# A fused attention block: the gate weight's eight factors summed on GpSimd instead of TensorE, under a newly written order of steps

## The chip, the cores and the metric

The kernel runs on one core of a Trainium2 chip. Its time is the device time of one execution in microseconds (us), the median over runs. The engines are TensorE (PE, matmuls), VectorE (DVE), ScalarE (ACT), GpSimd (POOL) and the DMA queues; each takes its instructions strictly in the order in which they are written and waits on semaphores.

## The reference

x has 4 batches of 512 rows of 256 numbers. What matters of it:

```python
xn = _layernorm(x, axis=-1)
qkv = xn @ Wqkv.T + bqkv          # 16 heads of 16; rotary embedding on q and k
att = softmax(causal(q @ k.T / 4)); s = (att @ v) @ Wo.T + bo
mixed = jnp.einsum('btd,rde->bte', xn, factors) / math.sqrt(8) + bias   # factors: 8 x 256 x 256
out = x + s * silu(mixed)
```

The einsum over r multiplies xn by the sum of the eight factors, so the kernel sums them once, at the start, into one 256x256 "gate weight".

## The kernel before

**Data.** All products with weights are made in two parts, a rounded high part (ACT copies it) and the rest (DVE or POOL subtracts): three products each. This holds for the weights of q and k (`wqk_sb`), of v and gate together (`wvg_sb`), of the output (`wo_sb`), for the normalised input (`xnT`) and for q and k themselves. Rotated q and k lie in `parts`; DMAs copy their high and low parts into stacked tiles `stack_q` and `stack_k`, whose free rows are filled by memsets beforehand (`fill`). For each batch the heads come in two units of eight.

**Steps.** For each batch: `stats` and `rstd` (mean and variance on DVE, the root on POOL), `normalise` (ACT; in batch 0 half on DVE), `turn_x` (PE transposes), `project_qk` (four steps of six products of 128x512), `rotate`, `high`, `low` and `stack` per unit, `project_vg` (four steps of six products), `maxima` (products for the row maxima, 40 chunks, reduced by DVE), `shift`, `scores` (products for the exponentials, taken by ACT), `values`, `take_o`, `turn_o`, `turn_y`, `project_o`, `store`.

**The gate weight.** Two DMAs load the factors into `fac`, a view of the tile `probs`, which is still free then. The step `sum_factors` adds the eight factors on PE by products with the identity into one PSUM bank; `split_gate` takes that bank: ACT writes the high part into `wvg_sb` (L910), DVE the rest (L792). `project_vg` of batch 0 needs both.

**The order.** `plan()` sorts the steps by the times written in the tables `CHAINS` (one row per batch), `MAXIMA`, `ATTENTION` and `END`. These times are only sort keys. Every engine walks the same sorted list and emits its own part of each step, so a step's place in the list sets what it stands behind on each engine. PSUM is used as a ring of eight banks in the order of the steps in `RING_KINDS`. `JOINED` names pairs of chunks whose masks are issued behind both chunks' products; `VALUES_AT` says at which chunk of the next group `values`, `take_o` and `turn_o` of a group stand.

**The stack of batch 0, unit 0.** It is filled through three queues (`FIRST_QUEUES`): the high and low parts of q by SP (step `stack` 0 and 1), the high part of k by POOL's queue (step `stack_gpsimd`), the low part of k by ACT's queue (step `stack_scalar`). These DMAs are issued by the engine itself at that place of its order. PE's first `maxima` waits for all of them (`wait_stack`):

```python
                eng.wait_ge(s_first_stack[0], 16 * first_dmas(SCALAR))
                eng.wait_ge(s_first_stack[1], 16 * first_dmas(GPSIMD))
            eng.wait_ge(s_stack[b % PARITIES][u], 16 * (STACK_DMAS * (b // PARITIES + 1) - others))
```

At the start PE runs 24 products of no use (`WARM_UP`, L570), and five more in `keep_warm` (L612).

Of the kernel before, what the change touches and what calls it, by code (L numbers as in the profile page):

```python
# [133 lines left out]
def attention_steps(b, g):  # L134

    s = []
    before = b * GROUPS + g - 1
    gb, gg = before // GROUPS, before % GROUPS
    for c in range(EXP_CHUNKS):
        s.append((c, ("scores", b, g * EXP_CHUNKS + c)))  # L140
        if before >= 0:
            s += [(c, (kind, gb, gg)) for kind, at in VALUES_AT if at == c]
    return s


def spread(steps, start, end):

    return [(start + (end - start) * (c // 2 * 2) / EXP_CHUNKS, step) for c, step in steps]


def shift_pairs(kind, b, u):
# [6 lines left out]
    (("stats", 0, -35.009), ("late_fill", 3, -22.829), ("rstd", 0, -21.238), ("keep_warm", 0, -14.711),  # L158
     ("split", 0, -14.601), ("normalise", 0, -14.545), ("fill", 0, -12.703), ("turn_x", 0, -11.842),
     ("turn_x", 1, -10.913), ("project_qk", 0, -10.001), ("split", 1, -9.814), ("fill", 1, -9.381),  # L160
     ("project_qk", 1, -9.255), ("rotate", 0, -9.216), ("stack_gpsimd", 0, -8.100), ("load", 1, -7.481),
     ("split", 2, -7.317), ("high", 0, -6.524), ("split", 3, -5.832), ("sum_factors", 0, -4.773),
     ("load", 2, -4.163), ("low", 0, -3.927), ("split_gate", 0, -2.954), ("stack_scalar", 1, -2.356),
     ("project_qk", 2, -2.146), ("fill", 2, -2.030), ("project_qk", 3, -1.952), ("rotate", 1, -1.795),
     ("stack", 0, -1.785), ("project_vg", 0, -1.389), ("high", 1, -0.567), ("project_vg", 1, -0.436),
     ("fill", 3, -0.397), ("low", 1, -0.384), ("project_vg", 2, -0.311), ("project_vg", 3, -0.259),
     ("stack", 1, 0.162), ("bias_vg", 0, 0.292), ("stack", 2, 0.735), ("first_shift", 0, 1.188),
     ("gate_tanh", 0, 1.232), ("shift", 0, 1.353), ("gate", 0, 1.431), ("stack", 3, 1.518), ("shift", 1, 1.896),
     ("turn_y", 0, 2.372), ("turn_y", 1, 2.604), ("project_o", 0, 2.816), ("project_o", 1, 2.903),
     ("load", 3, 3.163), ("store", 0, 4.465), ("store", 1, 7.296)),  # L170
    (("stats", 0, -6.753), ("rstd", 0, -3.783), ("normalise", 0, -1.479), ("turn_x", 0, 0.740), ("turn_x", 1, 0.776),
     ("project_vg", 0, 1.044), ("project_qk", 0, 1.089), ("project_qk", 1, 1.193), ("project_vg", 1, 1.225),
     ("project_vg", 2, 1.299), ("rotate", 0, 1.358), ("project_qk", 2, 1.522), ("project_qk", 3, 1.543),
     ("high", 0, 1.554), ("rotate", 1, 1.598), ("low", 0, 1.694), ("stack", 0, 1.705), ("project_vg", 3, 1.712),
     ("bias_vg", 0, 1.759), ("stack", 1, 1.867), ("gate_tanh", 0, 1.952), ("high", 1, 2.031), ("stack", 2, 2.043),
     ("low", 1, 2.173), ("shift", 0, 2.223), ("gate", 0, 2.292), ("stack", 3, 2.320), ("shift", 1, 3.016),
     ("turn_y", 0, 4.363), ("turn_y", 1, 4.820), ("project_o", 0, 5.177), ("project_o", 1, 5.617),
     ("store", 0, 12.675), ("store", 1, 13.830)),
    (("stats", 0, -1.348), ("rstd", 0, 0.743), ("normalise", 0, 1.650), ("turn_x", 0, 1.764), ("turn_x", 1, 1.774),
     ("project_qk", 0, 1.960), ("project_qk", 1, 1.985), ("project_qk", 2, 2.227), ("rotate", 0, 2.228),  # L180
     ("high", 0, 2.305), ("project_qk", 3, 2.315), ("stack", 0, 2.437), ("low", 0, 2.531), ("stack", 1, 2.635),
     ("rotate", 1, 3.021), ("project_vg", 0, 3.042), ("high", 1, 3.097), ("project_vg", 1, 3.223),
     ("project_vg", 2, 3.520), ("project_vg", 3, 3.563), ("low", 1, 3.580), ("bias_vg", 0, 3.581),
     ("shift", 0, 4.264), ("stack", 2, 4.352), ("gate_tanh", 0, 4.364), ("gate", 0, 4.716), ("stack", 3, 4.751),
     ("shift", 1, 5.306), ("turn_y", 0, 7.016), ("turn_y", 1, 7.279), ("project_o", 0, 7.661),
     ("project_o", 1, 7.690), ("store", 0, 16.049), ("store", 1, 22.818)),
# [927 lines left out]
```

## Time and profile before

| | |
|---|---|
| median of 3 runs | 225.77 us (225.0 to 225.97) |
| the profiled execution | 225.08 us, of which the span of its instructions is 223.3 us |
| PE busy | 210.4 us, 94% |
| DVE busy | 167.8 us, 75% |
| ACT busy | 137.9 us, 62% |
| POOL busy | 112.8 us, 51% |

The span runs from the first instruction to the last. A share of busy time is an average over stages that have different limits, so the stages at the start have to be read apart.

### The profile page before, as it was taken

The page shows a single profiled execution, that of the slowest core. Times are in us where ns is not written, and L with a number is a line of the kernel's source. Part 1 is how long each engine was busy: PE and PEld are TensorE (multiplying, and loading weights), DVE is VectorE, ACT ScalarE, POOL GpSimd, SP SyncE. Part 2 cuts the span into 40 slices and gives each one's busy share as a digit, 9 for nine tenths or more (in the row PEclk, how much of TensorE's full clock was granted, in tenths as well). Part 3 has the DMA queues.
Part 4 walks back from the last instruction along what each step waited for, and adds up shares of the span by engine and source line. Part 5 has one row for each costly group of instructions (what it writes and reads, how often), then busy time and mean ns, then how long its engine had stood idle before and what let it go on. Part 6 is the DMA issues. An engine that isn't in the chain of part 4 may idle for free.

```text
span 223.3 us, 5566 instructions
## 1 busy us (share of the span) xinstructions
PE 210.4 (94%) x2193; PEld 141.0 (63%) x2193; DVE 167.8 (75%) x268; ACT 137.9 (62%) x268; POOL 112.8 (51%) x104
## 2 busy tenths in 40 slices
PE   6999998998999999999999999999999999999892
PEld 2478866666657556667775575658756665585471
DVE  7779949979999797786976699669947796741233
ACT  2333461359664875893558978891278658869930
POOL 7884999753930860400779200954750034029912
PEclk9999999999999999999999999999999999999999
DMA  5996915101520340150036300035155000002002
GB/s 147 365 358 205 218 53 193 44 3 42 176 71 9 130 155 6 58 203 27 4 101 207 126 3 6 0 117 181 43 188 191 3 6 3 3 9 94 3 0 97
DMA packets 15790, 21.47 MB, mean 96 GB/s; under 512 B 2068, under 2 KB 9236, under 8 KB 15764
## 3 DMA queue, kind: packets, MB, share of 16 engines
q1 hardware_dynamic: 15248, 20.06, 27.5%
q0 software_dynamic: 192, 0.52, 1.0%
q10 hardware_dynamic: 324, 0.52, 0.8%
q8 instruction: 18, 0.29, 0.6%
q14 instruction: 8, 0.07, 0.1%
HBM read 6.16 MB, written 2.10 MB: 37 GB/s over the span
## 4 chain that ended last, share of the span: by engine, by line
PE 66%; DVE 18%; POOL 7%; ACT 4%; issue 4%; DVEq 0%; POOLq 0%
PE ring_ps L484 16%; DVE rowmax L832 10%; PE ring_ps L550 9%; PE ring_ps L521 9%; PE ring_ps L607 6%; PE ring_ps L626 5%; PE ring_ps L494 5%; PE ring_ps L502 5%; PE ring_ps L676 3%; PE ring_ps L642 2%; ACT probs L944 2%; PE ring_ps L681 2%; DVE parts L805 2%; PE ring_ps L583 1%; DVE by_sin L807 1%
## 5 line engine op out<-in xcount | busy, mean ns | idle before, releaser
L832 DVE TENSOR_REDUCE rowmax<-ring_ps 128x2 f32<-128x768 f32 (+3 forms) x103 | 89.5, 915 | 22.6 <-PE ring_ps L502 22.2
L944 ACT ACTIVATE probs<-ring_ps 128x512 f32<-128x512 f32 x160 | 83.5, 608 | 23.3 <-PE ring_ps L502 16.6
L484 PE MATMUL ring_ps<-probs,vaug 128*17 128x256 f32 (+3 forms) x528 | 37.8, 426 | 1.0 <-ACT probs L944 0.7
L521 PE MATMUL ring_ps<-stack_k,stack_q 62*128 62x512 f32 (+3 forms) x256 | 37.2, 355 | 1.6 <-DVE rowmax L832 0.6
L550 PE MATMUL ring_ps<-stack_q,stack_k 64*128 64x128 f32 (+3 forms) x256 | 36.4, 351 | 0.5
L502 PE MATMUL ring_ps<-ident_bf,masks 64*128 64x128 bf16 (+1 forms) x640 | 36.0, 210 | 0.0
L521 PEld LDWEIGHTS ring_ps<-stack_k,stack_q 62*128 62x128 f32 x256 | 20.9, 185 | 11.1 <-issue 7.8
L714 POOL TENSOR_TENSOR parts<-parts 128x1024 fp32r<-128x1024 f32 x7 | 16.7, 2381 | 21.9 <-ACT parts L915 21.9
L484 PEld LDWEIGHTS ring_ps<-probs,vaug 128*17 128x17 f32 x528 | 13.8, 97 | 22.0 <-issue 16.5
L550 PEld LDWEIGHTS ring_ps<-stack_q,stack_k 64*128 64x128 f32 x256 | 21.1, 185 | 8.9 <-issue 6.3
L626 PE MATMUL ring_ps<-wvg_sb,xnT 128*128 128x512 f32 x96 | 25.1, 405 | 1.2 <-DVE rowmax L832 0.8
L502 PEld LDWEIGHTS ring_ps<-ident_bf,masks 64*128 64x128 bf16 x640 | 17.7, 95 | 9.7 <-issue 5.5
L1073 POOL TENSOR_TENSOR result<-result,gate 128x512 f32<-128x512 f32 x6 | 7.7, 1282 | 30.0 <-DVE result L870 30.0
L607 PE MATMUL ring_ps<-xnT,wqk_sb 128*128 128x512 f32 x84 | 22.2, 405 | 0.0
L709 POOL TENSOR_TENSOR parts<-parts,by_sin 128x512 f32<-128x512 f32 x7 | 9.0, 1283 | 23.4 <-DVE by_sin L807 23.4
L626 PEld LDWEIGHTS ring_ps<-wvg_sb,xnT 128*128 128x128 f32 x96 | 17.2, 188 | 5.7 <-DVE rowmax L832 1.1
L1049 POOL TENSOR_TENSOR vaug<-vaug,bias_sb 128x512 f32<-128x512 f32 x8 | 9.4, 1194 | 17.3 <-ACT gate L926 17.3
L607 PEld LDWEIGHTS ring_ps<-xnT,wqk_sb 128*128 128x128 f32 x84 | 15.1, 188 | 3.4
L968 ACT ACTIVATE oT<-ring_ps 128x512 f32<-128x512 f32 x15 | 9.0, 598 | 9.1 <-PE ring_ps L484 9.0
L494 PE MATMUL ring_ps<-wo_sb,yT 128*128 128x256 f32 x96 | 13.6, 289 | 0.2 <-DVE yT L762 0.2
L915 ACT ACTIVATE parts<-parts 128x1024 fp32r<-128x1024 f32 x8 | 8.5, 1064 | 8.1 <-POOL parts L710 5.2
L925 ACT ACTIVATE vaug<-ring_ps 128x256 f32<-128x256 f32 x16 | 6.1, 384 | 11.8 <-PE ring_ps L626 7.5
(95 smaller groups left out, 279.3 us busy)
## 6 DMA issues: line engine op xcount, KB each, us to landing
stack_q<-parts SPq DMA_DIRECT2D x48, 128.0 KB, 2.6
stack_k<-parts SPq DMA_DIRECT2D x42, 128.0 KB, 2.6
probs<-factors SPq DMA_DIRECT2D x2, 1024.0 KB, 8.4
out<-result SPq DMA_DIRECT2D x8, 256.0 KB, 2.3
xbuf<-x SPq DMA_DIRECT2D x3, 512.0 KB, 8.3
xbuf<-x SPq DMA_DIRECT2D x2, 256.0 KB, 2.9
probs<-wqk SPq DMA_DIRECT2D x2, 256.0 KB, 4.6
stack_k<-parts POOLq DMA_DIRECT2D x4, 128.0 KB, 3.6
```

Of the source, the lines that this page charges most:

```text
L484: mm = pe.matmul(ps[32 * s:32 * s + HD + 1, first:end], vaug[:, b % 2, j, h, :], probs[:, slot, col + first - j * P:col + end - j * P], st ...
L494: mm = pe.matmul(ps[:, s * C:(s + 1) * C], yT[:, a, k, t * P:(t + 1) * P], wo_sb[:, m, k, :], start=(k == 0 and n == 0 and s == 0), stop=( ...
L502: return pe.matmul(diagonal[:, :, half * ROWS:(half + 1) * ROWS], masks[rows, of_maxima, half, :], own, start=False, stop=(half == 1))
L521: pe.matmul(ps[:, col:col + (tile + 1) * P], qk[b % 2][0][rows, h // SIDES, tile * P:(tile + 1) * P], qk[b % 2][1][rows, h // SIDES, 0:(ti ...
L550: pe.matmul(ps[:, col:col + T - j * P], qk[b % 2][1][side(h), h // SIDES, j * P:(j + 1) * P], qk[b % 2][0][side(h), h // SIDES, j * P:T], ...
L607: mm = pe.matmul(ps[:, :], wqk_sb[:, a, k, i * P:(i + 1) * P], xnT[:, m, k, :], start=(n == 0), stop=(n == len(products) - 1))
L626: mm = pe.matmul(ps[:, :], xnT[:, a, k, i * P:(i + 1) * P], wvg_sb[:, m, k, :], start=(n == 0), stop=(n == len(products) - 1))
L709: eng.tensor_tensor(rotated[i][:, 0, :], rotated[i][:, 0, :], by_sin[:, 1, :], ALU.subtract)
L714: eng.tensor_tensor(parts[:, i, 1], rotated[i], parts[:, i, 0].bitcast(F32), ALU.subtract).then_inc(rotary_signal(kind, b, i), 1)
L832: taking = dve.tensor_reduce(of_both, keys, AX_X, ALU.max)
L944: act.activation(probs[:, chunk % PROB_SLOTS, :], ps[:, :], ACT.Exp, scale=float(HD) ** -0.5).then_inc(taken[kind], 1)
L1049: last = pool.tensor_tensor(v, v, bias_v.unsqueeze(1).broadcast_to([P, QT, H // 2, HD]), ALU.add)
```

## The change

`sum_factors` leaves PE. POOL waits for both loads of the factors and adds them in `fac` itself: the last four to the first four, then two, then one (three instructions that each wait for the one before). It signals `s_summed`; ACT and DVE take the sum from SBUF instead of PSUM, and a new semaphore `s_gate_split` says that both parts are written. The ring of banks has one entry less. All the tables of the order are new, and `VALUES_AT` now has one row per group, so that `values`, `take_o` and `turn_o` may stand at another chunk in each.

```diff
-RING_KINDS = ("turn_x", "sum_factors", "project_qk", ...
+RING_KINDS = ("turn_x", "project_qk", ...
...
                 elif kind == "project_vg":
                     pe.wait_ge(taken["turn_x"], count("turn_x", b, KC - 1))
                     if b == 0 and i == 0:
                         pe.wait_ge(s_split, count("split", 0, 2))
-                        pe.wait_ge(taken["sum_factors"], 1)
+                        pe.wait_ge(s_gate_split, 1)
...
-                elif kind == "sum_factors":
-                    for k in range(KC):
-                        pe.wait_ge(s_fac[k], 16)
-                        for r in range(RANK):
-                            mm = pe.matmul(ps[:, k * C:(k + 1) * C], ident[:], fac[:, k, r, :],
-                                           start=(k == 0 and r == 0), stop=(k == KC - 1 and r == RANK - 1))
-                    mm.then_inc(done_pe[kind], 1)
...
-        summed = ring_bank(("sum_factors", 0, 0))[:, :].rearrange("p (k e) -> p k e", k=KC)
+        summed = fac[:, :, 0, :]
...
+                elif kind == "sum_factors":
+                    for k in range(KC):
+                        pool.wait_ge(s_fac[k], 16)
+                    half = RANK // 2
+                    while half > 1:
+                        after(pool.tensor_tensor(fac[:, :, 0:half, :], fac[:, :, 0:half, :],
+                                                 fac[:, :, half:2 * half, :], ALU.add))
+                        half //= 2
+                    pool.tensor_tensor(summed, summed, fac[:, :, 1, :], ALU.add).then_inc(s_summed, 1)
...
                 elif kind == "split_gate":
-                    act.wait_ge(done_pe["sum_factors"], 1)
+                    act.wait_ge(s_summed, 1)
                     act.activation(gate_split[:, 0], summed, ACT.Copy).then_inc(s_gate_high, 1)
```

```diff
-VALUES_AT = (("values", 3), ("take_o", 3), ("turn_o", 7))
+VALUES_AT = ((3.0, 5.1), (0.6, 9.5), (2.7, 5.0), (2.8, 4.6), (2.4, 8.5), (2.5, 6.0), (2.2, 9.5), (2.1, 6.6),
+             (3.8, 7.7), (2.6, 7.7), (2.0, 9.5), (0.5, 7.1), (3.9, 9.5), (3.2, 9.5), (4.8, 9.5))
```

What the tables move is seen in the order of the instructions. First ACT, from batch 0's high part of q and k, unit 0 (`parts`, L915 before and L908 after) on. `wvg_sb<-` is the high part of the gate weight, `xn<-` is `normalise` of batch 1, the second `parts<-` the high part of unit 1, and `DMA stack_k<-parts` is `stack_scalar`. Before:

```order
L915 ACTIVATE parts<-parts 128x1024 [waits first_rotate_ready]
L907 ACTIVATE wo_sb<-probs 128x512 [waits o_weights_loaded]
L910 ACTIVATE wvg_sb<-ring_ps 128x2x256 [waits pe_sum_factors]
L421 DMA stack_k<-parts 16x4x512 [waits stack_rows_set_k0,first_low_ready]
L421 DMA stack_k<-parts 16x4x512
L902 ACTIVATE xn<-xbuf,centre,rstd 128x256 [waits pe_turn_x,rstd_ready]
L902 ACTIVATE xn<-xbuf,centre,rstd 128x256 x3
L925 ACTIVATE vaug<-ring_ps 128x16x16 [waits pe_project_vg]
L926 ACTIVATE gate<-ring_ps 128x256
L915 ACTIVATE parts<-parts 128x1024 [waits rotate_ready]
```

After:

```order
L908 ACTIVATE parts<-parts 128x1024 [waits first_rotate_ready]
L903 ACTIVATE wvg_sb<-probs 128x2x256 [waits factors_summed]
L895 ACTIVATE xn<-xbuf,centre,rstd 128x256 [waits pe_turn_x,rstd_ready]
L895 ACTIVATE xn<-xbuf,centre,rstd 128x256 x3
L908 ACTIVATE parts<-parts 128x1024 [waits rotate_ready]
L421 DMA stack_k<-parts 16x4x512 [waits stack_rows_set_k0,first_low_ready]
L421 DMA stack_k<-parts 16x4x512
L918 ACTIVATE vaug<-ring_ps 128x16x16 [waits pe_project_vg]
```

The two DMAs of `stack_scalar` have moved from ahead of `normalise` 1 to behind it and behind the high part of unit 1.

Now POOL, from the last fills of batch 0 on; `fill` writes `stack_q` and `stack_k`, the four rows on `rstd` and `centre` are `rstd` of batch 1, `parts<-parts,by_sin` is `rotate` of unit 1, and the DMA is `stack_gpsimd`. Before:

```order
L428 MEMSET stack_k 128x1024 x3
L428 MEMSET stack_q 128x1024
L428 MEMSET stack_k 128x1024
L421 DMA stack_k<-parts 16x4x512 [waits stack_rows_set_k0,high_ready]
L421 DMA stack_k<-parts 16x4x512 x3
L1032 TENSOR_TENSOR wo_sb<-probs,wo_sb 128x512 [waits weights_high]
L1019 TENSOR_SCALAR rstd<-moments 128x4 [waits xn_ready,first_xn_ready,moments_ready]
L1020 TENSOR_TENSOR rstd<-rstd,minus_half 128x4 [waits pool_own]
L1021 TENSOR_TENSOR centre<-moments,rstd 128x4 [waits pool_own]
L1022 TENSOR_SCALAR centre<-centre 128x4 [waits pool_own]
```

After:

```order
L1032 TENSOR_TENSOR probs<-probs 128x2x1024 [waits factors_loaded1,factors_loaded0]
L1032 TENSOR_TENSOR probs<-probs 128x2x512 [waits pool_own]
L1035 TENSOR_TENSOR probs<-probs 128x2x256 [waits pool_own]
L428 MEMSET stack_q 128x1024
L428 MEMSET stack_k 128x1024
L421 DMA stack_k<-parts 16x4x512 [waits stack_rows_set_k0,high_ready]
L421 DMA stack_k<-parts 16x4x512 x3
L428 MEMSET stack_q 128x1024
L428 MEMSET stack_k 128x1024
L702 TENSOR_TENSOR parts<-parts,by_sin 128x512 [waits taken_project_qk]
L703 TENSOR_TENSOR parts<-parts,by_sin 128x512
L1012 TENSOR_SCALAR rstd<-moments 128x4 [waits xn_ready,first_xn_ready,moments_ready]
```

The three sums stand ahead of two fills and `stack_gpsimd`, and `rstd` of batch 1 now stands behind another two fills and `rotate` of unit 1. The split of `wo_sb` has gone to a place behind these rows.

Last PE, from the products of batch 0 up to its first `maxima` (L521); L607 is `project_qk`, L626 before and L619 after `project_vg`. Before:

```order
L617 MATMUL ring_ps<-probs,ident 128x256 [waits factors_loaded0]
L617 MATMUL ring_ps<-probs,ident 128x256 x7
L617 MATMUL ring_ps<-probs,ident 128x256 [waits factors_loaded1]
L617 MATMUL ring_ps<-probs,ident 128x256 x7
L607 MATMUL ring_ps<-xnT,wqk_sb 128x512 [waits taken_turn_x,weights_split]
L607 MATMUL ring_ps<-xnT,wqk_sb 128x512 x5
L607 MATMUL ring_ps<-xnT,wqk_sb 128x512 [waits taken_turn_x]
L607 MATMUL ring_ps<-xnT,wqk_sb 128x512 x5
L626 MATMUL ring_ps<-wvg_sb,xnT 128x512 [waits taken_sum_factors,weights_split,taken_turn_x]
```

After:

```order
L607 MATMUL ring_ps<-xnT,wqk_sb 128x512 [waits taken_turn_x,weights_split]
L607 MATMUL ring_ps<-xnT,wqk_sb 128x512 x5
L607 MATMUL ring_ps<-xnT,wqk_sb 128x512 [waits taken_turn_x]
L607 MATMUL ring_ps<-xnT,wqk_sb 128x512 x5
L619 MATMUL ring_ps<-wvg_sb,xnT 128x512 [waits gate_weights_split,weights_split,taken_turn_x]
L619 MATMUL ring_ps<-wvg_sb,xnT 128x512 x5
```

PE's 16 products of the sum are gone and nothing else has moved between these rows; the remaining 18 products of `project_vg` and then the first `maxima` follow in both.

## Rows read from the trace of the kernel before

**Rows 1.** The page: busy time, share of the span and instructions of each engine.

```profile
PE 210.4 (94%) x2193; PEld 141.0 (63%) x2193; DVE 167.8 (75%) x268; ACT 137.9 (62%) x268; POOL 112.8 (51%) x104
```

**Rows 2.** Stretch, its length, busy us of PE, PEld, DVE, ACT, POOL, granted clock, DMA.

```profile
14.30:30.00 15.70, 15.70 (x72) 12.94 (x71) 12.95 (x31) 5.56 (x11) 11.00 (x16) 1.00 0.74 209
30.00:60.00 30.00, 26.95 (x242) 18.80 (x242) 27.31 (x35) 17.82 (x38) 22.43 (x19) 1.00 0.27 90
60.00:206.00 146.00, 143.43 (x1687) 95.09 (x1685) 112.46 (x174) 101.53 (x196) 59.53 (x43) 1.00 0.23 75
```

**Rows 3.** Timeline of PE from 8 us; start, length, instruction, idle before.

```profile
14.57 7.07 PE L617 MATMUL ring_ps<-probs,ident 128*128 128x256 f32 x32
21.29 3.08 PE L607 MATMUL ring_ps<-xnT,wqk_sb 128*128 128x512 f32 x12
24.21 5.77 PE L626 MATMUL ring_ps<-wvg_sb,xnT 128*128 128x512 f32 x24
29.90 0.50 PE L521 MATMUL ring_ps<-stack_k,stack_q 62*128 62x512 f32 x2
...
32.62 0.50 PE L521 MATMUL ring_ps<-stack_k,stack_q 62*128 62x384 f32 x4 [0.44 <-ACT gate L926]
```

**Rows 4.** The first line's DMAs on ACT's queue (`stack_scalar`).

```profile
L421 ACTq DMA_DIRECT2D stack_k<-parts x2: 647/1076/1506, 22.3 to 22.9; - x2
...
DMA to landing us min/median/max: 4.9/5.0/5.0
```

**Rows 5.** The loads of the factors.

```profile
L443 SPq DMA_DIRECT2D probs<-factors x2: 434/508/583, 4.2 to 4.7; - x2
...
DMA to landing us min/median/max: 7.1/8.4/9.6
```

**Rows 6.** Timeline of POOL.

```profile
10.24 3.64 POOL L428 MEMSET stack_k<- 128x1024 f32 x4 [0.52 <-DVE xn L779]
...
20.00 2.24 POOL L421 DMA_DIRECT2D stack_k<-parts  x4 [4.34 <-ACT parts L915]
...
23.66 0.19 POOL L1019 TENSOR_SCALAR rstd<-moments 128x4 f32<-128x4 f32 x1
...
25.35 0.19 POOL L1022 TENSOR_SCALAR centre<-centre 128x4 f32<-128x4 f32 x1
...
27.29 1.29 POOL L709 TENSOR_TENSOR parts<-parts,by_sin 128x512 f32<-128x512 f32 x1
...
31.57 2.38 POOL L714 TENSOR_TENSOR parts<-parts 128x1024 fp32r<-128x1024 f32 x1
```

**Rows 7.** Timeline of ACT.

```profile
18.65 1.06 ACT L915 ACTIVATE parts<-parts 128x1024 fp32r<-128x1024 f32 x1 [2.91 <-DVE parts L710]
...
21.67 0.60 ACT L910 ACTIVATE wvg_sb<-ring_ps 128x512 fp32r<-128x512 f32 x1 [1.45 <-PE ring_ps L617]
...
25.58 2.08 ACT L902 ACTIVATE xn<-xbuf,centre,rstd 128x256 f32<-128x256 f32 x4 [3.30 <-POOL centre L1022]
```

**Rows 8.** Timeline of DVE.

```profile
15.28 0.68 DVE L787 TENSOR_TENSOR wqk_sb<-probs,wqk_sb 128x512 fp32r<-128x512 f32 x1
...
19.13 1.40 DVE L771 BATCH_NORM_STATS2 stats<-xbuf 128x6 f32<-128x256 f32 x4
...
21.02 1.21 DVE L714 TENSOR_TENSOR parts<-parts 128x1024 fp32r<-128x1024 f32 x1
...
23.05 0.75 DVE L805 SCALAR_TENSOR_TENSOR parts<-ring_ps,bqk_sb,cos_t 128x512 f32<-128x512 f32 x1
...
24.41 0.75 DVE L805 SCALAR_TENSOR_TENSOR parts<-ring_ps,bqk_sb,cos_t 128x512 f32<-128x512 f32 x1
```

**Rows 9.** The page's DMA issues: KB each, median us to landing.

```profile
stack_q<-parts SPq DMA_DIRECT2D x48, 128.0 KB, 2.6
```

**Rows 10.** Timeline of PE's weight loads, first 9 us.

```profile
4.84 0.15 PEld L570 LDWEIGHTS ring_ps<-ident_bf 128*128 128x128 bf16 x1 [0.28 <-issue]
5.14 3.12 PEld L570 LDWEIGHTS ring_ps<-ident_bf 128*128 128x128 bf16 x15 [0.15 <-issue]
```

More of the change, by code:

```diff
@@ L134, in attention_steps @@
 def attention_steps(b, g):
-    s = []
+    s = [(c // 2 * 2, ("scores", b, g * EXP_CHUNKS + c)) for c in range(EXP_CHUNKS)]
     before = b * GROUPS + g - 1
[L138 to L143, printed above, removed]
+    if before >= 0:
+        values_at, turned_at = VALUES_AT[before]
+        which = divmod(before, GROUPS)
+        s += [(values_at, ("values",) + which), (values_at, ("take_o",) + which), (turned_at, ("turn_o",) + which)]
+    return sorted(s, key=lambda entry: entry[0])
 def spread(steps, start, end):
-    return [(start + (end - start) * (c // 2 * 2) / EXP_CHUNKS, step) for c, step in steps]
+    return [(start + (end - start) * at / EXP_CHUNKS, step) for at, step in steps]
 def shift_pairs(kind, b, u):
@@ L157 @@
 CHAINS = (
[L158 to L186, printed above, removed]
@@ new lines @@
+    (("stats", 0, -0.323), ("rstd", 0, 0.267), ("normalise", 0, 1.648), ("turn_x", 0, 1.760), ("turn_x", 1, 1.768),
+     ("project_qk", 0, 1.997), ("project_qk", 1, 2.038), ("rotate", 0, 2.121), ("project_qk", 2, 2.218),
+     ("high", 0, 2.314), ("project_qk", 3, 2.354), ("rotate", 1, 2.371), ("low", 0, 2.387), ("stack", 0, 2.601),
+     ("high", 1, 2.682), ("stack", 1, 2.837), ("project_vg", 0, 3.070), ("project_vg", 1, 3.317),
+     ("project_vg", 2, 3.554), ("project_vg", 3, 3.585), ("low", 1, 3.677), ("bias_vg", 0, 3.802),
+     ("stack", 2, 4.173), ("shift", 0, 4.271), ("gate_tanh", 0, 5.090), ("stack", 3, 5.382), ("shift", 1, 5.402),
+     ("gate", 0, 5.431), ("turn_y", 0, 6.996), ("turn_y", 1, 7.307), ("project_o", 0, 7.435),
+     ("project_o", 1, 7.595), ("store", 0, 14.768), ("store", 1, 20.305)),
@@ new lines @@
+    (("stats", 0, 3.722), ("rstd", 0, 3.906), ("normalise", 0, 4.012), ("turn_x", 0, 4.250), ("turn_x", 1, 4.253),
+     ("project_qk", 0, 4.464), ("project_qk", 1, 4.494), ("rotate", 0, 4.639), ("high", 0, 4.728), ("low", 0, 5.053),
+     ("project_qk", 2, 5.187), ("project_qk", 3, 5.239), ("rotate", 1, 5.279), ("high", 1, 5.556),
+     ("stack", 0, 5.684), ("stack", 1, 5.937), ("project_vg", 0, 6.290), ("project_vg", 1, 6.320), ("low", 1, 6.489),
+     ("project_vg", 2, 6.656), ("shift", 0, 6.841), ("project_vg", 3, 6.928), ("bias_vg", 0, 7.313),
+     ("shift", 1, 7.337), ("gate_tanh", 0, 7.702), ("turn_y", 0, 7.947), ("stack", 2, 11.152), ("gate", 0, 14.094),
+     ("stack", 3, 14.514)))
@@ L353, in block_kernel @@
         s_high = sem("high_ready")
+        s_summed = sem("factors_summed")
         s_gate_high = sem("gate_weights_high")
+        s_gate_split = sem("gate_weights_split")
         s_first_stack = [sem("first_stack_by_scalar"), sem("first_stack_by_gpsimd")]
@@ L940, in _ @@
                         act.wait_ge(s_last_split, 1)
[L941 removed]
+                        act.wait_ge(s_gate_split, 1)
                     if chunk >= PROB_SLOTS and i % (EXP_CHUNKS // 2) == 0:
```

67 lines of the change are left out of this document (39 added, 28 removed).

## The prediction

> **What bounds the kernel now.** I read the page's busy shares first, then the busy time by stretch, then the timelines of all engines over the first 35 us, since the sum of the factors stands there. PE is busy for 210.4 us, 94% of the span [rows 1], and where it stands still matters more than how long it works. From 14.3 to 30 us it is busy for 15.70 of 15.70 us; from 30 to 60 it idles 30.00 - 26.95 = 3.05 us, and from 60 to 206 only 146.00 - 143.43 = 2.57 us [rows 2]. So PE is the limit nearly throughout, with DVE close to it from 30 to 60 (27.31 of 30 us busy). In the first stretch PE runs the factors' products for 7.07 us, `project_qk` 2 and 3 for 3.08 us and `project_vg` for 5.77 us, back to back, and then goes into the first `maxima` at 29.90 [rows 3]. Is it at that moment that the stack is only just there? No: the last DMA of `stack_scalar` was issued at 22.9 and landed 5.0 us later, at 27.9 [rows 4]. The stack had 2.0 us of slack under 7.07 us of products on PE. These two numbers are the key: taking the products away can bring at most 2.0 us unless the stack also comes earlier, and whatever delays the stack by more than 2.0 us now costs time.
>
> **The change, part by part.** I walk each engine through its new order with durations of before; times are on the clock of the profiled execution.
>
> *PE.* The 7.07 us go. `project_qk` 2 waits for the second weight split on DVE, which ends at 15.28 + 0.68 = 15.96 [rows 8]. It and step 3 then run to about 16.0 + 3.1 = 19.1. After that `project_vg` waits for the gate weight.
>
> *POOL.* Its memsets end at 10.24 + 3.64 = 13.9 [rows 6], and the second half of the factors lands at 4.7 + 9.6 = 14.3 [rows 5]. The three sums work on 2048, 1024 and 512 elements per partition. The trace has the last two sizes: 2.38 us and 1.29 us [rows 6], a slope of 1.09 us per 512 elements. So 2048 elements should take 2.38 + 2 x 1.09 = 4.6 us, an extrapolation; the bare slope without a fixed part gives 4.4, two instructions of 2.38 us give 4.8, so it is narrow. Sum: 4.6 + 2.4 + 1.3 and about 0.2 for the two waits on itself = 8.5 us, done at 22.8. Behind it stand two fills (0.91 each, 3.64 for four [rows 6]), to 24.6; `stack_gpsimd`, whose input (`rotate` on DVE done at 19.2, then 1.06 us on ACT [rows 7]) is ready at 20.3, so that it takes only its own 2.24 us, to 26.9, against 20.0 to 22.2 before [rows 6]; two more fills, to 28.7; `rotate` of unit 1, 2 x 1.29 less overlap = 2.5, to 31.2; `rstd` of batch 1, 25.35 + 0.19 - 23.66 = 1.9 us [rows 6], to 33.1. Before, that `rstd` was done at 25.5.
>
> A rule speaks against this place. While POOL sums, DVE runs four operations with two inputs in SBUF (two splits and the two of `rotate`), each of the size of L787 at 0.68 us [rows 8]. No row that I found shows POOL slowed beside DVE, and I put in nothing; if POOL stood still under all four, the chain would be 4 x 0.68 = 2.7 us later, which I keep for the upper end. The Trainium skill (GPSIMD Engine Reference, Key points) says that GpSimd shares its SBUF interfaces with VectorE and that they contend when a DVE instruction has two SBUF inputs; it gives no price.
>
> *DVE.* The second split, `project_qk` 1, the third split and `rotate` take it to 19.2 as before; `stats` of batch 1 (1.40 and a short aggregation) to 21.0 [rows 8]. Then come `project_qk` 2 and 3, 24.41 - 23.05 = 1.36 us each, to 23.8, `low` of unit 0 (1.21) to 25.0 [rows 8], and the rest of the gate weight. ACT's high part of it follows the sum: 22.8 + 0.6 = 23.4 [rows 7]. So the gate weight is complete at 25.0 + 0.7 = 25.7, and PE's `project_vg` runs from 25.8 to 31.5 instead of 24.2 to 30.0. That alone would be +1.5 us: the sum on POOL plus the new order gives back all of the 7.07 us as a wait of 6.7 us on PE.
>
> *ACT, the decisive term.* Its two DMAs of `stack_scalar` stood right behind `low`, at 22.3. In the new order they stand behind `normalise` 1 and the high part of unit 1. `normalise` 1 waits for `rstd` at 33.1 and takes 2.08 us, to 35.2; `high` takes 1.06, to 36.2 [rows 7]. The second DMA is then issued at about 36.9, against 22.9 [rows 4]. Landing took 5.0 us there, with POOL's four DMAs and SP's issued from 20 us on just ahead of it [rows 6], and 2.6 us as the median over all of SP's stack DMAs [rows 9]. At 36.2 SP also issues unit 1's high parts, but nothing else is under way; I take 3.6, between the two, and get a complete stack at 40.5 (39.5 to 41.9). PE's first `maxima`, 29.90 before, starts at 40.5: **+10.6 us**. What is queued behind that wait on PE is everything: the transposes of batch 1, all maxima and scores. In front of it PE has nothing from 31.5 on.
>
> *What is made good afterwards.* By 40.5 ACT is through with most copies of `project_vg`, on which PE's ring of banks waited before: 0.44 us in one place [rows 3]. At the best all idle time of PE up to 206 us, 3.05 + 2.57 = 5.6 us [rows 2], vanishes; at the worst none. But DVE is 91% busy there from 30 to 60 and has the same work to do after the wait, so most of those waits will return. I take 1.6 us.
>
> *TensorE's clock.* The granted clock is 1.00 in every stretch of before [rows 2]. Yet at the start the weight loads of equal products come 0.43 us apart, and from 5.14 us on 15 of them in 3.12 us, 0.21 apart [rows 10]: the first 3.3 us ran at half the pace, the lower level of 1.2 GHz. The new order makes PE stand still twice, for 6.7 and for 9.0 us. After the first, a slow `project_vg` is hidden by the second. After the second, 3.3 us at half pace do 1.65 us of work less; DVE waits are mixed in there, so the cost is between 0 and 1.65. I take 1.0. The Trainium skill (TensorE: Matmul & The Clock Gate, Part 1) says that an idle PE falls back to 1.2 GHz and needs sustained work to return; by that rule the term would be its full 1.65.
>
> *The rest.* The ring loses an entry, DVE's reductions number 103 in place of 101 instructions, `JOINED` has 34 entries in place of 41, and `VALUES_AT` spreads `values` over the chunks. With 2.57 us of idle PE in 146 us there is nothing to gain beyond what is already counted; a bad place costs some tenths of a us each. I put in 0, with -1 to +2 for the range. The load of x for batch 2 moves behind SP's six stack DMAs, to about 26.3, and is needed by `stats` 2 ahead of DVE's first reduction. Its landing, were it as slow as the factors' 9.6 us, is at 35.9, with 1.9 us of `stats` behind it 37.8, still under the 40.5.
>
> **The sum.** +10.6 - 1.6 + 1.0 = +10.0 us on a profiled execution of 225.08 us: 235.1 us. That execution lies 0.7 us under the median of 225.77, so the median may come out a little above; I say 235.0.
>
> **The rivals.**
>
> *A, forecast, 0.78.* The stack of unit 0 comes late through ACT's order: 235, on its own 231 to 239.
>
> *B, the delay is absorbed, 0.08.* The same late start, but PE recovers all its idle time of 5.6 us since everything else has run ahead, and pays no clock: +10.6 - 5.6 = +5.0, 230. For it: 7.07 us of work have left PE, and POOL, ACT and SP get ahead during the wait. Against it: DVE has nothing to do ahead either.
>
> *C, not slower, 0.06.* One mechanism: the DMAs of `stack_scalar` don't hold PE up, only the gate weight does, with +1.5 us less 1.6 us made good, 225. The point from which it decides: the last of them must be issued by 31.5 - 5.0 = 26.5, so `rstd` 1 by about 23, 10 us sooner than I walk it. If the sum on POOL were so quick that the gate weight was no wait either, the whole 7.07 us would come out: 218. The order of ACT speaks against both: even with a sum of 0 us, `stack_gpsimd` can't start before 20.3, and the chain of 2.2 + 1.8 + 2.5 + 1.9 + 2.1 + 1.1 us behind it brings the second DMA to about 32.6, still 9.7 us later than before.
>
> *D, worse, 0.08.* The contention of 2.7 us, a landing of 5.0 us and the full clock penalty together, or a deadline missed in a later batch: +10.6 + 2.7 + 1.4 + 0.6 - 1.6 + 1.0 is +14.7, 240.
>
> **How the numbers follow.** 235.0 is A. The range reaches from B's 230 to just under D, 239.5; outside are C, D and A's edges, some 0.2. A change of about 0.5% (1.1 us) is what this measurement can tell from none. Slower by more: A, B and D, 0.94. C splits into 0.03 within 0.5% and 0.03 faster.
>
> **What would show it.** In the profile after: POOL's three sums at about 14.3, 4.6, 2.4 and 1.3 us long; PE idle from 19 to 25.8 behind DVE's split of the gate weight, and again from 31.5 to 40.5 until the first L521; ACT's DMA issues at 36 and 37 behind `normalise` and the high part; from there the same stretches as before, 10 us later; PE's busy total at some 203 to 205 us, 7.07 less plus the slow products. Wrong would be: a first L521 before 36 us (the walk of POOL or ACT is off), or one at 40 with an end before 228 (more is made good than PE's idle time). A POOL sum above 5.5 us would show the contention.

## The result, and the profile after

The changed kernel takes 233.31 us (median of 4 runs, 232.74 to 234.46) against 225.67 us: a ratio of 1.0347, 95% interval 1.0318 to 1.0376, so 7.6 us slower. The profiled execution took 232.74 us.

The page of the changed kernel, span and busy time, to be held against [rows 1]:

```profile
span 230.9 us, 5507 instructions
...
PE 207.1 (90%) x2161; PEld 138.4 (60%) x2161; DVE 172.7 (75%) x270; ACT 137.0 (59%) x268; POOL 122.0 (53%) x107
```

PE is busy for only 3.3 us less, though 7.07 us of products went: `project_qk` 2 and 3 and `project_vg` took 1.95 and 1.60 us longer at a fallen clock (below). The stretches of [rows 2], after (the last three columns are the granted clock, the DMA share and GB/s):

```profile
14.30:30.00 15.70, 5.99 (x17) 4.12 (x15) 15.49 (x21) 2.21 (x3) 14.38 (x11) 0.71 0.39 117
30.00:60.00 30.00, 26.91 (x180) 19.18 (x180) 22.00 (x36) 14.09 (x32) 22.43 (x22) 0.93 0.32 103
60.00:206.00 146.00, 142.15 (x1678) 95.81 (x1678) 118.60 (x181) 100.03 (x195) 59.49 (x42) 1.00 0.24 79
```

From 14.3 to 30 us PE was busy throughout before; now it works for 5.99 us, and its granted clock falls to 0.71 on average. PE's timeline, as in [rows 3]:

```profile
19.81 5.03 PE L607 MATMUL ring_ps<-xnT,wqk_sb 128*128 128x512 f32 x12 [4.55 <-DVE wqk_sb L780]
31.04 7.37 PE L619 MATMUL ring_ps<-wvg_sb,xnT 128*128 128x512 f32 x24 [6.20 <-DVE wvg_sb L785]
38.67 0.49 PE L521 MATMUL ring_ps<-stack_k,stack_q 62*128 62x512 f32 x2 [0.27 <-DMA stack_k<-parts]
```

The first `maxima` starts at 38.67 instead of 29.90: 8.8 us late. From there to the end of the span it takes 230.9 - 38.67 = 192.2 us, before 223.3 - 29.90 = 193.4. So the loss arises ahead of the first maxima, and 1.2 us of it is made good behind.

The first of PE's waits was forecast as about 1 us, up to 16.0; it is 4.55 us. The second, ahead of `project_vg`, is 6.20 us (forecast 6.7), and of the 9.0 us forecast ahead of the first `maxima` 0.27 are left. DVE and POOL over the same time:

```profile
15.80 3.95 DVE L780 TENSOR_TENSOR wqk_sb<-probs,wqk_sb 128x512 fp32r<-128x512 f32 x1
19.68 0.74 DVE L798 SCALAR_TENSOR_TENSOR parts<-ring_ps,bqk_sb,cos_t 128x512 f32<-128x512 f32 x1
...
20.99 1.54 DVE L780 TENSOR_TENSOR wvg_sb<-probs,wvg_sb 128x512 fp32r<-128x512 f32 x1
22.45 1.76 DVE L702 TENSOR_TENSOR parts<-parts,by_sin 128x512 f32<-128x512 f32 x1
24.14 0.68 DVE L703 TENSOR_TENSOR parts<-parts,by_sin 128x512 f32<-128x512 f32 x1
```

```profile
14.69 7.29 POOL L1032 TENSOR_TENSOR probs<-probs 128x2048 f32<-128x2048 f32 x2 [0.88 <-DMA probs<-factors]
22.06 1.61 POOL L1035 TENSOR_TENSOR probs<-probs 128x512 f32<-128x512 f32 x1
```

The two merged sums are 4.51 and 2.70 us long, so the first ends at 14.69 + 4.51 = 19.20. DVE's second weight split starts at 15.80 and ends at 19.75, 0.55 us after it: it took 0.68 us in [rows 8] and 3.95 now. I call this extra time of a DVE instruction beside one of GpSimd a hold. The two DVE operations of 1.54 and 1.76 us likewise end some 0.55 us behind the ends of the second and third sum. L798, which reads PSUM, takes its usual 0.74 us.

And ACT, at the place of the two stack DMAs:

```profile
35.26 0.60 ACT L895 ACTIVATE xn<-xbuf,centre,rstd 128x256 f32<-128x256 f32 x1 [8.83 <-POOL centre L1015]
35.32 0.64 ACTq L421 DMA_DIRECT2D stack_k<-parts  x1
35.77 0.59 ACT L895 ACTIVATE xn<-xbuf,centre,rstd 128x256 f32<-128x256 f32 x1
35.99 0.74 ACTq L421 DMA_DIRECT2D stack_k<-parts  x1
36.26 1.08 ACT L895 ACTIVATE xn<-xbuf,centre,rstd 128x256 f32<-128x256 f32 x2
37.24 1.04 ACT L908 ACTIVATE parts<-parts 128x1024 fp32r<-128x1024 f32 x1
```

The DMAs stand behind L895 and L908 in ACT's order, yet they are issued at 35.32, as soon as `rstd` is there, while both still have to run. They wait for the semaphores of what stands ahead, not for its execution. (e1, e5, e8 and e13, which keep these DMAs at this place, show the same, 0.07 us behind the start of the first L895 or its like.)

Which chain ended last ahead of the first `maxima`? The view of it (start, length, what; shortened):

```profile
15.89 3.86 DVE wqk_sb L780
...
24.85 1.07 ACT parts L908
...
26.21 0.72 POOL stack_k L421
...
30.30 1.73 POOL parts L702
...
33.34 0.20 POOL rstd L1012
...
35.99 2.64 DMA stack_k<-parts
```

It is the chain to the stack, through DVE's held split, the high part, `stack_gpsimd`, two fills, `rotate` of unit 1 and `rstd` on POOL to ACT's last DMA. The other chain, over the gate weight and `project_vg`, ended at 31.04 + 7.37 = 38.41, only 0.26 us sooner.

### The profile page after: what moved, and what is told of

Read it like the earlier page. It is cut to its first block, busy times and chain, and to the rows that moved or that the text cites. A ratio compares the mean times of both kernels' runs of the same rounds, so it can differ in the third digit from the quotient of the medians.

```text
span 230.9 us, 5507 instructions
## 1 busy us (share of the span) xinstructions
PE 207.1 (90%) x2161; PEld 138.4 (60%) x2161; DVE 172.7 (75%) x270; ACT 137.0 (59%) x268; POOL 122.0 (53%) x107
## 4 chain that ended last, share of the span: by engine, by line
PE 61%; DVE 17%; POOL 7%; issue 5%; ACT 4%; DMA 3%; ACTq 1%; DVEq 0%; POOLq 0%
PE ring_ps L484 15%; DVE rowmax L825 11%; PE ring_ps L550 10%; PE ring_ps L521 8%; PE ring_ps L607 5%; PE ring_ps L502 5%; PE ring_ps L494 4%; PE ring_ps L570 3%; PE ring_ps L669 3%; DMA stack_q<-shift 2%; PE ring_ps L619 2%; DVE wqk_sb L780 2%; ACT probs L937 2%; PE ring_ps L674 1%; POOL parts L702 1%
## 5 line engine op out<-in xcount | busy, mean ns | idle before, releaser
L825 DVE TENSOR_REDUCE rowmax<-ring_ps 128x2 f32<-128x1024 f32 (+3 forms) x101 | 87.3, 909 | 19.5 <-PE ring_ps L502 16.4
L550 PE MATMUL ring_ps<-stack_q,stack_k 64*128 64x128 f32 (+3 forms) x256 | 37.3, 358 | 2.9 <-DMA stack_q<-shift 0.9
L521 PE MATMUL ring_ps<-stack_k,stack_q 62*128 62x512 f32 (+3 forms) x256 | 36.7, 353 | 1.1 <-DVE rowmax L825 0.4
L502 PE MATMUL ring_ps<-ident_bf,masks 64*128 64x128 bf16 (+1 forms) x640 | 37.2, 210 | 0.0
L619 PE MATMUL ring_ps<-wvg_sb,xnT 128*128 128x512 f32 x96 | 26.4, 423 | 6.7 <-DVE wvg_sb L785 6.2
L607 PE MATMUL ring_ps<-xnT,wqk_sb 128*128 128x512 f32 x84 | 23.8, 431 | 5.2 <-DVE wqk_sb L780 4.5
L521 PEld LDWEIGHTS ring_ps<-stack_k,stack_q 62*128 62x128 f32 x256 | 21.1, 186 | 9.1 <-issue 5.6
L619 PEld LDWEIGHTS ring_ps<-wvg_sb,xnT 128*128 128x128 f32 x96 | 18.5, 201 | 11.7 <-issue 6.6
L502 PEld LDWEIGHTS ring_ps<-ident_bf,masks 64*128 64x128 bf16 x640 | 18.2, 95 | 10.5 <-issue 5.5
L702 POOL TENSOR_TENSOR parts<-parts,by_sin 128x512 f32<-128x512 f32 x7 | 9.5, 1351 | 27.0 <-DVE by_sin L800 27.0
L607 PEld LDWEIGHTS ring_ps<-xnT,wqk_sb 128*128 128x128 f32 x84 | 16.5, 206 | 9.6 <-DVE wqk_sb L780 5.0
L908 ACT ACTIVATE parts<-parts 128x1024 fp32r<-128x1024 f32 x8 | 8.6, 1070 | 13.1 <-DVE parts L703 8.9
```

The costliest lines, as they stand in the source:

```text
L502: return pe.matmul(diagonal[:, :, half * ROWS:(half + 1) * ROWS], masks[rows, of_maxima, half, :], own, start=False, stop=(half == 1))
L521: pe.matmul(ps[:, col:col + (tile + 1) * P], qk[b % 2][0][rows, h // SIDES, tile * P:(tile + 1) * P], qk[b % 2][1][rows, h // SIDES, 0:(ti ...
L550: pe.matmul(ps[:, col:col + T - j * P], qk[b % 2][1][side(h), h // SIDES, j * P:(j + 1) * P], qk[b % 2][0][side(h), h // SIDES, j * P:T], ...
L607: mm = pe.matmul(ps[:, :], wqk_sb[:, a, k, i * P:(i + 1) * P], xnT[:, m, k, :], start=(n == 0), stop=(n == len(products) - 1))
L619: mm = pe.matmul(ps[:, :], xnT[:, a, k, i * P:(i + 1) * P], wvg_sb[:, m, k, :], start=(n == 0), stop=(n == len(products) - 1))
L702: eng.tensor_tensor(rotated[i][:, 0, :], rotated[i][:, 0, :], by_sin[:, 1, :], ALU.subtract)
```

## The experiments

Each is compared with the kernel before on its own chip; the ratio's 95% interval stands behind it.

**e1, the sums cut small.** In the changed kernel each level of the sum is made of instructions of 512 elements.

```diff
+                        for k in range(KC):
+                            for r in range(0, half, 2):
+                                last = pool.tensor_tensor(fac[:, k, r:r + 2, :], fac[:, k, r:r + 2, :],
+                                                          fac[:, k, half + r:half + r + 2, :], ALU.add)
+                        after(last)
```

> The changed kernel, with GpSimd's sums cut into instructions of 512 elements per partition (seven in all, instead of one of 2048, one of 1024 and one of 512). Theory H (a DVE instruction with two inputs in SBUF can't start while a two-input GpSimd instruction is under way, and stands still for the whole rest of it): DVE's second weight split, 3.95 us long in the changed kernel, comes down to at most 1.3 + 0.7 = 2.0 us, and PE's project_qk 2 starts at about 17.8 instead of 19.8. Rival S (the two engines share the port and both run slower over the whole overlap): the split stays at 3 us or more. By both GpSimd's sum ends later, at about 25 to 26 instead of 23.7 (7 x 1.28 us and the holds), and with it the chain to the first maxima, so the total is 232.5 to 236.

233.65 us, 1.0371 (1.0339 to 1.0404). DVE and PE in it:

```profile
16.00 1.61 DVE L780 TENSOR_TENSOR wqk_sb<-probs,wqk_sb 128x512 fp32r<-128x512 f32 x1
...
18.86 1.68 DVE L780 TENSOR_TENSOR wvg_sb<-probs,wvg_sb 128x512 fp32r<-128x512 f32 x1
20.46 1.77 DVE L702 TENSOR_TENSOR parts<-parts,by_sin 128x512 f32<-128x512 f32 x1
22.15 1.75 DVE L703 TENSOR_TENSOR parts<-parts,by_sin 128x512 f32<-128x512 f32 x1
```

```profile
17.67 4.61 PE L607 MATMUL ring_ps<-xnT,wqk_sb 128*128 128x512 f32 x12 [2.22 <-DVE wqk_sb L780]
```

The hold shrinks with GpSimd's instruction, as theory H says: 3.95 becomes 1.61, and now all four two-input operations are held once. The total does not move. The sum ends later, at 25.03 instead of 23.67 us, but POOL no longer waits for the high part (0.76 us) and `rotate` of unit 1 is no longer held (1.29 us instead of 1.78), so `rstd` comes at 35.30 as against 35.22, and the first maxima, behind the stack, at 38.61. `project_vg` ended 0.53 us before that.

**e2, the stack DMAs early on ACT, in the changed kernel.**

```diff
-     ("split_gate", 0, -2.373), ("stack", 0, -2.200), ("high", 1, -2.013), ("stack_scalar", 1, -1.832),
+     ("stack_scalar", 1, -2.374), ("split_gate", 0, -2.373), ("stack", 0, -2.200), ("high", 1, -2.013),
```

> The changed kernel with one step moved: the two DMAs of stack_scalar stand ahead of the gate weight's high part and of normalise 1 on ACT, instead of behind normalise 1 and the high part of unit 1. Theory of the prediction (the place of these DMAs sets the first maxima by itself): the first maxima comes at about 34 instead of 38.67 and the time falls by 4 us or more. Rival (PE's project_vg ends at 38.4, only 0.3 us before the stack is there, so the DMAs were one of two equal terms): the first maxima comes at about 38.4 and the time falls by 0.3 us, 233.

235.24 us, 1.0451 (1.042 to 1.0482): slower than the changed kernel, which neither side expected. ACT now stands at the DMAs until `low` is there and only then reaches the gate weight:

```profile
30.64 1.45 ACTq L421 DMA_DIRECT2D stack_k<-parts  x2
...
32.13 0.63 ACT L903 ACTIVATE wvg_sb<-probs 128x512 fp32r<-128x512 f32 x1 [5.91 <-issue]
...
33.77 7.17 PE L619 MATMUL ring_ps<-wvg_sb,xnT 128*128 128x512 f32 x24 [9.27 <-DVE wvg_sb L785]
```

The high part of the gate weight goes from 25.81 to 32.13 and `project_vg` from 31.04 to 33.77. The stack was early and of no use. But the move did two things at once, so this run gives no price for the place of the DMAs alone. That is read from the changed kernel's own rows: `project_vg` ended at 38.41, so an earlier stack could bring 0.3 us there at most.

**e3, the old order, only the sum moved to GpSimd.** The kernel before with the diff's code and with `("sum_factors", 0, -9.382)` just ahead of the second fill.

> The kernel before with nothing changed but the sum: on GpSimd, in the place that it has in the changed kernel (ahead of the second fill). Order of ACT, DVE and the other tables as before. Theory H (DVE held by GpSimd's sums): DVE's second split takes about 4 us again, the gate weight and low part come some 6 us late, first maxima at about 36 instead of 29.9, total 230 to 232. Rival P (the new order of ACT and GpSimd, as predicted, is what costs): first maxima at 30 to 31.5, total 225 to 227.

233.61 us, 1.037 (1.0353 to 1.0388). DVE's second split takes 3.86 us and the first maxima comes at 37.67. The move of the sum alone costs what the whole change costs. That is more than theory H had, and the rows show two things that H did not name: the clock fell in both waits (e7), and a fourth DVE instruction was held, the rest of the gate weight, beside POOL's split of `wo_sb`:

```profile
27.71 1.95 DVE L787 TENSOR_TENSOR wvg_sb<-probs,wvg_sb 128x512 fp32r<-128x512 f32 x1
27.83 1.27 POOL L1027 TENSOR_TENSOR wo_sb<-probs,wo_sb 128x512 fp32r<-128x512 f32 x1
```

**e5, the new order, the sum on PE.** The changed kernel with PE's loop and `("sum_factors", 0, -7.463)`.

> The changed kernel's order with the sum back on PE (behind project_qk 1, in the ring of banks). Theory H: no DVE instruction is held, the second split takes 0.7 us; PE is busy without a gap until about 31 us; what is left is the late rstd and stack_scalar: the first maxima at about 35, total 228 to 230. Rival P (the new order is nearly all of the loss): first maxima at 37 or later, total 231 or more.

230.77 us, 1.0245 (1.0224 to 1.0266), between the two. The first maxima comes at 35.91. PE was not free of gaps, as theory H had it: it waited 3.33 us ahead of `project_vg` for DVE, which in the new order takes `project_qk` 2 and 3 before the rest of the gate weight, and `project_vg` then took 7.18 us. The new order alone costs 5.4 us; with e3's 8.2 us that would make 13.6, and the change costs 7.6. The two delays lie side by side, not one behind the other.

**e8 and e9, the new order piece by piece.** Both start from e5.

```diff
+     ("high", 0, -5.231), ("low", 0, -5.230), ("split_gate", 0, -5.229), ("project_qk", 2, -5.228),
...
+     ("stack_scalar", 1, -5.229),      # e9 only, in place of -1.832
```

The first line is e8's; in e9 `split_gate` has -5.2292, so that `stack_scalar` stands behind it.

> e5 (the new order with the sum on PE, 230.8 us) with low of unit 0 and the split of the gate weight ahead of project_qk 2 and 3 on DVE, as in the old order; ACT's stack_scalar stays late. PE then has no gap ahead of project_vg, which runs at 25.2 to 31. Theory of the prediction (the late rstd and stack_scalar hold the first maxima by themselves): first maxima at about 35 (e5: 35.9), total 229.5 to 230.5. Rival (the wait for the gate weight on DVE was what cost): first maxima at 31 to 32, total 226 to 227.

> e8, and the two DMAs of stack_scalar on ACT right behind the gate weight's high part, ahead of normalise 1. Theory of the prediction: the stack is complete at about 29, the first maxima comes at 31, when project_vg ends, total 225 to 226. Rival (something else of the new order in batch 0, such as GpSimd's late rstd, is still waited for): first maxima at 33 or later, 227.5 or more.

e8: 230.14 us, 1.0199 (1.0147 to 1.0251), in time as the prediction's theory had it; the first maxima comes at 33.69, sooner than its 35, after 3.7 us of waiting for the stack:

```profile
24.18 5.77 PE L624 MATMUL ring_ps<-wvg_sb,xnT 128*128 128x512 f32 x24
33.69 0.79 PE L519 MATMUL ring_ps<-stack_k,stack_q 62*128 62x512 f32 x2 [3.74 <-DMA stack_k<-parts]
```

With the sum on PE, then, the late stack of the forecast is a wait of its own. The four runs lie at 228.8 and 228.9 and at 231.4 and 231.7 us; the profiled one is of the upper pair, so e8 doesn't tell itself from e5 in time, only by its rows. e9: 228.73 us, 1.013 (1.0114 to 1.0145). The first maxima is back at 30.24, but PE's second transpose is not:

```profile
34.40 1.97 PE L581 MATMUL ring_ps<-ident,xn 128*128 128x128 f32 x8 [3.19 <-ACT gate L924]
```

ACT's copies of `project_vg` wait behind `normalise` 1, which waits for the late `rstd`. That was e9's rival. The clock fell in e8's wait and in e9's (0.50 from 34 to 40 us in both), so part of both totals is slow products.

**e6, the old start, the new rest.** The sum on PE, batch 0's row of `CHAINS` as before, all other tables new.

> The sum on PE and the first row of CHAINS (batch 0) as before; all the other tables (CHAINS of batches 1 to 3, MAXIMA, ATTENTION, END, JOINED, VALUES_AT) as in the changed kernel. From the first maxima to the end the changed kernel took 192.2 us and the kernel before 193.4. Theory of the start (all of the loss arises ahead of the first maxima, the new tables behind it are slightly better): first maxima at 29.9 as before, 224.3 us, 0.5% faster. Rival (the new tables only did well because everything was ahead after the long wait): 225.5 to 227.

228.43 us, 1.0126 (1.0105 to 1.0148): above the theory's value and above the rival's range too, so neither holds as it was put. Behind an unchanged start PE meets one wait of 2.83 us, after which the granted clock was 0.50 from 47 to 53 us:

```profile
47.51 1.01 PE L640 MATMUL ring_ps<-ident,rowmax 128*4 128x128 f32 x4 [2.83 <-DVE rowmax L830]
48.17 2.91 PE L624 MATMUL ring_ps<-wvg_sb,xnT 128*128 128x512 f32 x6
```

In the kernel before, a `project_vg` step stood in front of that transpose. My reading, which no run tests: keys of two tables that were not made together sort into an order that neither had. So this run tells nothing of the new rest by itself.

**e7, e3 with PE kept busy.** 18 products of no use ahead of `project_qk` 2 and 28 ahead of `project_vg`.

> The old order with the sum on GpSimd (e3, 233.6 us), and in PE's two idle stretches 18 and 28 products of no use, ahead of project_qk 2 and ahead of project_vg. In e3 project_qk 2 and 3 took 5.07 us and project_vg 7.93 us, against 3.08 and 5.77 before, at a granted clock of 0.50 in most of those stretches, and the first maxima came at 37.67, when project_vg ended. Theory (the clock that falls in the waits is a cost of its own): both come back to 3.1 and 5.8 us, the first maxima at about 35.6, total 231.5. Rival (those products were slow for another reason, or the rest waits for the stack or for DVE anyway): 233 or more.

231.78 us, 1.0271 (1.0253 to 1.0289), 1.8 us less than e3.

```profile
19.89 3.02 PE L609 MATMUL ring_ps<-xnT,wqk_sb 128*128 128x512 f32 x12 [0.85 <-DVE wqk_sb L782]
...
29.96 5.82 PE L621 MATMUL ring_ps<-wvg_sb,xnT 128*128 128x512 f32 x24 [0.99 <-DVE wvg_sb L787]
...
35.70 0.50 PE L523 MATMUL ring_ps<-stack_k,stack_q 62*128 62x512 f32 x2
```

`project_vg` comes back from 7.93 to 5.82 us and the first maxima from 37.67 to 35.70. In e3 the fallen clock cost these 2.0 us.

**e13, the changed kernel with PE kept busy**, by 18 and 26 such products.

> The changed kernel (233.3 us) with 18 products of no use on PE ahead of project_qk 2 and 26 ahead of project_vg, nothing else. Theory of two nearly equal terms (in the changed kernel project_vg ended at 38.4 and the last stack DMA landed at 38.6): project_vg comes back from 7.37 to 5.8 us and ends at about 36.9, but the first maxima still starts at 38.4 to 38.7, behind the DMA of stack_scalar, total 232.8 to 233.3. Rival (PE's clock alone holds the start): first maxima at 37, total 231.5.

232.8 us, 1.0329 (1.0295 to 1.0364). The first maxima stays at 38.65. But the 26 products ended 2.6 us before `project_vg` could start, and it took 7.39 us again (the granted clock was 0.59 from 32 to 34). So the run never had the quick `project_vg` that it was made for, and is inconclusive, though time and first maxima are as the theory had them.

**e10, GpSimd busy without reading.** e3 with eight memsets of 1024 elements in place of the sum. It leaves the sum out: the gate weight is the first factor alone.

> The old order with GpSimd's step in the same place as in e3 (233.6 us), but its three sums are replaced by eight memsets of 1024 elements in the upper factors, each waiting for the one before: GpSimd is busy for nearly the same time (about 8.2 us) without reading anything. It leaves the sum out: the gate weight is the first factor alone. Theory H (in e3 the cost is DVE held by two-input GpSimd instructions, not GpSimd's own time): DVE's second split takes 0.7 us, the high part of unit 0 comes at 19.7 instead of 24.2, project_vg starts at 24.2 to 24.5 at a fallen clock, first maxima at 31.5 to 32, total 227 to 228. Rival O (GpSimd's occupation delays the rest of its queue and that is the cost): 231 to 234, as e3.

231.05 us, 1.0244 (1.0213 to 1.0275): in time at the lower edge of rival O's range, and well above theory H's 227 to 228. The first maxima, at 33.00, lies between what H expected and e3's.

```profile
15.51 0.68 DVE L782 TENSOR_TENSOR wqk_sb<-probs,wqk_sb 128x512 fp32r<-128x512 f32 x1
15.72 7.02 POOL L1033 MEMSET probs<- 128x1024 f32 x7 [1.63 <-DMA probs<-factors]
...
17.54 0.69 DVE L704 TENSOR_TENSOR parts<-parts,by_sin 128x512 f32<-128x512 f32 x1
```

```profile
25.27 7.80 PE L621 MATMUL ring_ps<-wvg_sb,xnT 128*128 128x512 f32 x24 [6.02 <-DVE wvg_sb L787]
33.00 0.50 PE L523 MATMUL ring_ps<-stack_k,stack_q 62*128 62x512 f32 x2
...
36.94 1.12 PE L585 MATMUL ring_ps<-ident,xn 128*128 128x128 f32 x4 [2.38 <-ACT gate L921]
```

DVE is not held by a memset (0.68 and 0.69 us), and the first maxima comes 4.7 us sooner than in e3. But 2.38 us return at PE's transpose, behind the late `rstd` and `rotate` in GpSimd's queue. The memsets end at 23.74, as e3's sum did at 23.63, so GpSimd is occupied for as long. Of e3's 8.2 us, then, 5.5 (4.8 to 6.2) come without any hold, with PE's waits in them and the clock (`project_vg` took 7.80 us), and about 2.7 are the holds net. Theory H, by which the holds were the cost, is refuted for the larger part.

**e11 and e12, a quarter of the sum on GpSimd.** The kernel before, with one addition of 1024 elements before any two-input DVE operation is due; in e12 the third fill also stands behind `rotate` 1.

```diff
+                elif kind == "half_sum":
+                    pool.wait_ge(s_fac[0], 16)
+                    pool.tensor_tensor(fac[:, 0, 0:4, :], fac[:, 0, 0:4, :], fac[:, 0, 4:8, :], ALU.add
+                                       ).then_inc(s_half_sum, 1)
...
+                        ranks = RANK // 2 if k == 0 else RANK
```

> The kernel before with one GpSimd addition of 1024 elements, at about 11.4 to 13.8 us, ahead of DVE's second weight split: the last four factors of the first half are added to the first four, so that PE's sum has 12 products instead of 16 (5.3 us instead of 7.07). No DVE operation with two inputs in SBUF is under way then. Theory (PE's work ahead of the first maxima is the limit there, with 2.0 us of slack in the stack): first maxima at 28.2, the time falls by up to 1.7 us, 224.0. Rival (PE then waits for ACT, whose copies of project_vg stand behind the high part of unit 1, which waits for GpSimd's rotate at 29.8): the gain is lost at PE's second transpose, 225.3 to 225.8.

> e11, and GpSimd's third fill behind rotate of unit 1 instead of ahead of it, so that rotate is 1.8 us earlier, at 25.5 to 28.0, and with it the high part of unit 1 and ACT's copies of project_vg. Theory (the rival of e11 is right, and this removes its wait): 224.0 to 224.5. If the place of this wait is elsewhere: the same as e11.

e11: 225.97 us, 1.0021 (0.9999 to 1.0043). e12: 224.53 us, 0.9962 (0.9947 to 0.9977), the only one below the kernel before. In e11 PE's sum takes 5.34 us and the second transpose waits 1.21 us for ACT; in e12 that wait is gone and the stack is the limit:

```profile
14.88 5.34 PE L621 MATMUL ring_ps<-probs,ident 128*128 128x256 f32 x24
...
29.86 0.49 PE L522 MATMUL ring_ps<-stack_k,stack_q 62*128 62x512 f32 x2 [0.75 <-DMA stack_k<-parts]
```

The last DMA to land for it was SP's low part of q, issued at 23.3 and landed 6.4 us later, at 29.7. e12's profiled execution, 225.28 us, lies above its median, so its rows don't show where the 1.0 us lies; nor was the fill's new place run without the addition.

## Why the prediction was right

The time, 233.3 us, and the direction are as forecast (235.0, range 230.0 to 239.5), and of rival A this much happened: the first maxima waits for the stack, which is late through POOL's and ACT's order, and the rest is as before. The way there is partly another one, and that the number came so close is in part luck: the stack's time was put together from one term 2.1 us too small (`rstd`) and two that were 3.0 and 1.0 us too large, and a second chain that the forecast let end 9.0 us sooner arrived 0.3 us before it.

*The slack of the stack.* I took 2.0 us from the DMAs on ACT's queue, landed at 27.9. But the stack is also filled by SP, whose last DMA for it landed later:

```profile
L421 SPq DMA_DIRECT2D stack_q<-parts x1: 1509/1509/1509, 23.0 to 23.0; - x1
...
DMA to landing us min/median/max: 5.4/5.4/5.4
```

That is 28.4 (23.0 + 5.4), so the slack was 1.5 us. The sum of the forecast doesn't hang on it.

*The sum on POOL.* Forecast 4.6, 2.4 and 1.3 us from 14.3 to 22.8; measured 4.51, 2.70 and 1.61 from 14.69 to 23.67. The sizes hold, the last two with a wait for DVE in them.

*The contention, put in as nothing.* This step failed. I asked whether POOL would stand still under DVE and kept 2.7 us for it. That no row of before showed it proved nothing: there no DVE instruction with two inputs in SBUF fell beside a POOL instruction that reads more than 4 elements per partition. It is DVE that stands still, for the rest of a whole POOL instruction: 3.3 + 0.9 + 1.1 us over the usual lengths. With it the high part of unit 0 came at 24.85 instead of 19.2, and the gate weight was complete at 30.9 instead of 25.7. Of the three, the first also kept PE waiting for 4.55 us ahead of `project_qk` 2, at 19.81 instead of 16.0. My sign for it, a POOL sum above 5.5 us, looked at the wrong engine: the longest was 4.51 us. The rule of the Trainium skill (GPSIMD Engine Reference, Key points) that I quoted was right; the trace gives it its form and price.

*ACT as the decisive term.* Half right. DMAs were counted as waiting for `normalise` and `high` to run (3.1 us); they wait only for `rstd`. It came at 35.2 instead of 33.1: the sum ended 0.9 us later than forecast, POOL waited 0.8 us for the high part, and `rotate` of unit 1 was 0.5 us longer beside DVE's split of the gate weight. The DMAs came at 35.3 and 36.0 instead of 36.2 and 36.9, and landed in 2.6 us, not 3.6: 38.6 instead of 40.5. That two late terms met there, `project_vg` ending at 38.4 and the stack at 38.6, I had not seen, so the place of the DMAs alone was worth 0.3 us at most. With the sum on PE, it does hold the stack (e8).

*"A slow project_vg is hidden by the second wait."* Wrong: it ran for 7.37 us, at a clock of 0.50 until 34 us, and ended with the stack. In exchange the second wait was 0.27 us, and the +1.0 us for the maxima is 0: the granted clock was 1.00 from 36 us on. PE's busy total, forecast as 203 to 205 us, is 207.1 for the slow products.

*Made good afterwards.* 1.6 us forecast, 1.2 us measured. The sum of the terms was +10.0 and is 8.8 - 1.2 = +7.6; what was too large is the landing, ACT's 3.1 us and the clock, what was missing is the hold.

*Rival C* needed `rstd` 1 by about 23; it came at 35.2. Even without any hold (e10) the time is 5.5 us above before. *D* added the contention to all other terms; it came without them.

Open is how much of the changed kernel's 8.8 us each cause has. e3, e5, e8 and e10 show that several delays of 4 to 8 us lie side by side, so that removing one gives back little. No run takes the holds alone out of the changed kernel (e1 trades them for a longer sum). An estimate from its rows: on the chain to the stack they are POOL's wait of 0.76 us for the high part, 0.5 us of `rotate`, and 0.3 us in each of the last two sums, 1.9 us in all. The other 7 us or so are then what the forecast walked, POOL's occupation and the order behind it.

## What to carry to other kernels

Before work goes to GpSimd, list the VectorE instructions that fall into its time and have two inputs in SBUF: each can be late by the rest of one GpSimd instruction, so such work goes where none is due (e11, e12). Cutting it small shortened each hold but not the kernel (e1). And count GpSimd's time itself: without any hold it still cost 5.5 us (e10). Work taken off the limiting engine gives back only the slack of what it waits for next, here 1.5 us of 7.07 by the rows of the kernel before (e12, with 1.7 us taken off PE, gained 1.0), and whatever is queued behind the moved work on its new engine has to be walked too. On ACT, a DMA issue waited for the semaphores of what stood ahead, not for its execution (issued at 35.32 while what stood ahead ran until 38.28), and itself stopped all behind it until its own wait was over (e2).
